# Graph network on one core: the logarithms of the edge counts are stored as they are computed, and the attention layers fetch them in pieces of 500 bytes

## The chip, the cores and the metric

The kernel runs on one core of one Trainium2 chip. The metric is the time of one execution in microseconds (us), as the device measures it. The unchanged kernel took 5342.97 us (median of 3 runs, 5340.74 to 5346.93).

## The reference

A graph of 3125 nodes with 256 features and 100,000 edges runs through two layers. Each layer has graph attention (four attentions in all), a linear attention, and a mixture of experts. What matters here is how every graph attention uses the edges:

```python
loop = jnp.arange(N)
src, dst = jnp.concatenate([src, loop]), jnp.concatenate([dst, loop])
e = leaky_relu(a_src[src] + a_dst[dst], 0.2)          # one number for each edge and head
ee = jnp.exp(e - segment_max(e, dst)[dst])
alpha = ee / (segment_sum(ee, dst)[dst] + 1e-16)
out = segment_sum(h[src] * alpha[:, :, None], dst)    # for each target node
```

An edge can occur several times, and each node has an edge to itself. The first attention has 4 heads of 64 features, the second and third 4 heads of 128, the fourth one head of 256.

## The kernel before

The kernel treats the graph as dense. It counts once how often each source node (3125) is tied to each target node (3125), and stores for each pair the negated logarithm of the count (a huge number where the count is 0) in the matrix `lowered` in device memory, `m.NL`, 3125 x 3125 float32, 39 MB. Node numbers are split as N = 3125, R = 125 rows to a tile, T = 25 tiles; W5 = 5.

*The counts stage* (`stage_counts`) goes through 25 tiles of 125 target nodes. For a tile it handles 25 windows of 5 target nodes. VectorE writes one-hot matrices (L303, four comparisons a tile), TensorE multiplies them (L317, L320) into PSUM banks, ScalarE takes the logarithm (L336) and a marker for zero (L337), and VectorE subtracts the two (L296) into `nl`, one of two buffers. There partition p stands for one of the window's five target nodes and one of 25 blocks of sources (p = 25 e + s), and along the row lie the 25 windows w with 125 sources b each. SyncE then stores `nl` with `tile_dma` (L65 for 112 partitions, L66 for the other 13) through the view `m.NLQ`. The view puts each run of 125 numbers (500 bytes) where a plain matrix has it: target node 5 (25 t + w) + e, sources 125 s + b. ScalarE may write into a buffer again when its store has landed (semaphore `nl_out`).

*The attention stages* (`stage_gat_attend`; in the trace g0a, g1a, g2a, g3a) go over the 25 tiles of target nodes, for two heads at a time (g3: one). So g0, g1 and g2 go through the tiles twice, g3 once: 50 + 50 + 50 + 25 = 175 fetches. A unit is one tile and one head. For a unit VectorE adds the scores (L932) into one of three buffers `x`, then adds the fetched rows `nl` and takes the minimum of each row in one instruction (L937, seen as CUSTOM_DVE_ANT_0), ScalarE takes exponentials (L991), TensorE transposes (L1102), ScalarE copies (L999), and TensorE gathers with the features (L1115). GpSimd finishes the rows; in g1 and g2 it stores them to `attended`.

`nl` has two buffers, for tiles of even and odd number. `counts` in the SyncE program of the stage fetches one tile: 125 rows of 12,500 bytes, one for each target node, on semaphore `nl_in`, which rises by 32 for the two transfers. SyncE issues the first two fetches at the start of the stage, and the fetch for tile t + 2 when both heads of tile t have been masked (semaphore `masked`). VectorE waits for `nl_in` ahead of L937 on the first head of a tile, after L932. SyncE does nothing else in these stages.

The order of work is written out by hand. The queues are in program order on each engine; all engines meet between stages.

Of the kernel before, what the change touches and what calls it, by code (L numbers as in the profile page):

```python
# [11 lines left out]
ds = bass.ds  # L12

N = 3125
R = 125
T = N // R
# [46 lines left out]
def tile_dma(eng, dst, src, sem):  # L63

    eng.dma_start(dst[0:CUT], src[0:CUT]).then_inc(sem, 16)  # L65
    eng.dma_start(dst[CUT:R], src[CUT:R]).then_inc(sem, 16)  # L66


def wait_apart(eng, tick, sem, value):

    eng.wait_ge(sem, value)
    eng.sem_inc(tick, 1)
# [20 lines left out]
W5 = 5  # L93
# [727 lines left out]
TURN = 6  # L821


def stage_gat_attend(nc, m, g, AL, HX, OUT, X=None, spare=None):
# [5 lines left out]
    H, F, HG = g.heads, g.feat, min(g.heads, 2)  # L830
# [3 lines left out]
    with Stage(nc, g.name + "a") as s:  # L834
        als, nl = s.sb("als", [R, H, N]), s.sb("nl", [R, 2, N])
# [10 lines left out]
        nl_in = [s.sem(f"nl_in{p}") for p in range(2)]  # L846
# [19 lines left out]
        def unit(q, i, k):  # L866
            return q * UT + i * BODY + k

        def tile_of(q, i, k):
            return q * T + i * TURN + k // HG  # L870

        def ahead(q, i, k, n):
            k += n
            if isinstance(i, int):
                at = i * BODY + k
                if at >= UT:
                    q, at = q + 1, at - UT
                i, k = at // BODY, at % BODY
                if i >= LOOPED:
                    i, k = LOOPED, at - LOOPED * BODY  # L880
            return q, i, k

        def exists(q, i, k, n):
            return not isinstance(i, int) or q * UT + i * BODY + k + n < PASSES * UT

        def before_all(q, i, k):
            return isinstance(i, int) and tile_of(q, i, k) < 0

        def ring(q, k):
            return (q * UT + k) % 3  # L890
# [7 lines left out]
        def units(eng, step, peeled=False):  # L898
            for q in range(PASSES):
                if q == 0 and peeled:  # L900
                    for k in range(BODY):
                        step(0, 0, k)
                with eng.Fori(1 if q == 0 and peeled else 0, LOOPED) as i:
                    for k in range(BODY):
                        step(q, i, k)
                for k in range(UT - LOOPED * BODY):
                    step(q, LOOPED, k)

        @block.sync
        def _(sp):  # L910
            def counts(gt, p):
                t = gt - gt // T * T if isinstance(gt, int) else gt
                tile_dma(sp, nl[:, p, :], m.NL[ds(t * R, R)], nl_in[p])
            counts(0, 0)
            counts(1, 1)
            for q in range(PASSES):
                with sp.Fori(0, T // 2 - 1) as i:
                    for p in range(2):
                        wait_apart(sp, s.tick, masked, (q * T + i * 2 + p + 1) * HG)
                        counts(i * 2 + p + 2, (q + p) % 2)  # L920
                for t in range(T - 3, T):
                    if q * T + t + 2 < PASSES * T and (t == T - 3 or q < PASSES - 1):
                        sp.wait_ge(masked, (q * T + t + 1) * HG)
                        counts(q * T + t + 2, (q + t) % 2)

        @block.vector
        def _(dve):
            def score(q, i, k):
                b, j, t = ring(q, k), k % HG, i * TURN + k // HG
                h = q * HG + j  # L930
                dve.wait_ge(turned, unit(q, i, k) * NG + NG)
                nc.vector.scalar_tensor_tensor(out=x[:, b, :], in0=als[:, h, :], scalar=cd[:, h:h + 1, ds(t, 1)].rearrange("p a b -> p (a b)"),  # L932
                                               in1=as2[:, j, :], op0=ALU.add, op1=ALU.min)
                nc.vector.drain()
                if j == 0:
                    wait_apart(dve, s.tick, nl_in[(q + k // HG) % 2], (i * TURN // 2 + (q * T + k // HG) // 2) * 32 + 32)
                nc.vector.tensor_tensor_reduce(out=x[:, b, :], in0=x[:, b, :], in1=nl[:, (q + k // HG) % 2, :], scale=1.0, scalar=3e38,  # L937
                                               op0=ALU.add, op1=ALU.min, accum_out=top[:, b:b + 1])
                nc.vector.drain().then_inc(masked, 1)  # L939

            def first(q, k):
                if q == 0:
                    dve.wait_ge(als_ready, (k + 1) * NG)
                    nc.vector.tensor_scalar(as2[:, k, :], als[:, k, :], 0.2, None, ALU.mult)
                    nc.vector.drain()
                else:
                    dve.wait_ge(scaled, (q - 1) * HG + k % HG + 1)
                score(q, 0, k)

            def invert(q, i, k):  # L950

                p = (q + k // HG) % 2
                dve.wait_ge(copied, (tile_of(q, i, k) + 1) * HG + 2)
                nc.vector.reciprocal(rec[:, p, :], raw[:, p, :, F]).then_inc(inverted, 1)

            dve.wait_ge(offset_ready, 1)
            for k in range(2):
                if k < HG:
                    first(0, k)
                else:  # L960
                    score(0, 0, k)
            dve.sem_inc(copied, 2)

            def step(q, i, k):
                if exists(q, i, k, 2):
                    nq, ni, nk = ahead(q, i, k, 2)
                    if nq > q and nk < HG:
                        first(nq, nk)
                    else:
                        score(nq, ni, nk)  # L970
                if (k - 2) % HG == HG - 1 and not before_all(q, i, k - 2):
                    invert(q, i, k - 2)
            units(dve, step, True)
            left = UT - LOOPED * BODY
            for k in range(left, left + 2):
                if (k - 2) % HG == HG - 1:
                    invert(PASSES - 1, LOOPED, k - 2)
# [1430 lines left out]
def build(nc, a, out):  # L2408
    m = Machine()
    m.src, m.dst = a["src"], a["dst"]  # L2410

    def dram(name, shape, dt=F32):
        return nc.dram_tensor(name, shape, dt).ap()
    m.QB = dram("edge_codes", [EDGES + CAP, 2])
    m.LO = dram("window_starts", [25, 25], I32)
    m.NL = dram("lowered", [N, N])
    m.NLQ = m.NL.rearrange("d s -> (d s)").rearrange("(t w p b) -> p t w b", t=T, w=T, p=R)
    m.XR, m.YR = dram("routed_rows", [SLOTS, D]), dram("expert_rows", [SLOTS, D])
    m.Y, m.XS = dram("attended", [N, 512]), dram("kept_rows", [R, T, D])
    with ExitStack() as ctx:  # L2420
# [150 lines left out]
```

## Time and profile before

| | before |
|---|---|
| median of 3 runs | 5342.97 us |
| lowest to highest | 5340.74 to 5346.93 us |
| profiled execution | 5338.39 us |
| its span | 5336.7 us |
| counts stage, first to last store issued | 174.6 to 446.7 us |
| g0 attention, first fetch to last mask | 926 to 1773 us |
| g1 and g2 | 2740 to 3572, 3729 to 4562 us |
| g3 | 4667 to 4992 us |
| busy in the span | TensorE 85%, VectorE 60%, ScalarE 53%, GpSimd 28% |

Times in rows of the profile are counted from the span's start. PE is TensorE's multiplications, PEld its loading of weights, DVE VectorE, ACT ScalarE, POOL GpSimd, SP SyncE; a q behind an engine's name means its sequencer, where transfers are issued. The DMA share is the mean busy share of the core's 16 DMA engines, and it can read slightly over 1. A row of windows gives the stretch, its length, the busy time of PE, PEld, DVE, ACT and POOL in this order with the number of instructions, TensorE's granted clock as a share of full speed, the DMA share and the GB/s moved. A row of the timeline gives start, duration, engine, line, operation, output and inputs, and in brackets the idle time before it and what ended it; of a tile's view, the shortest/median/longest duration in ns and the first and last start.

### The profile page before, as it was taken

What the parts mean: (1) busy time and instruction counts of PE and PEld (TensorE: products, weight loads), DVE (VectorE), ACT (ScalarE), POOL (GpSimd) and SP (SyncE); (2) the same over time, 40 slices, a digit from 0 to 9 for tenths busy, and PEclk for the clock granted to TensorE, in tenths of its full rate; (3) what the DMA queues carried; (4) which work ended last, traced back from release to release, by engine and by line L of the source; (5) the groups of instructions that cost most, each with busy time, mean ns of one, the idle gap of its engine ahead of it and who ended that gap; (6) DMA issues with size and microseconds to landing.
All of it is one profiled execution on the core that took longest, in us unless ns stands there. A gap on an engine that the chain in (4) does not pass through costs nothing. (4 is left out here: it accounts for less than half of the span.)

```text
span 5336.7 us, 91286 instructions
## 1 busy us (share of the span) xinstructions
PE 4535.1 (85%) x33942; PEld 4121.6 (77%) x33942; DVE 3198.2 (60%) x2773; ACT 2849.9 (53%) x3865; POOL 1473.4 (28%) x1158
## 2 busy tenths in 40 slices
PE   1554769999999629992979999997999999789989
PEld 1443447999999619991569999996999999778755
DVE  4896230788888521114458888862888888355333
ACT  0563322677777404431237787771777877344332
POOL 3001000122222040004016666660466666200000
PEclk9877769899999759996989999998999999899989
DMA  2583010333333045552024444422444344354100
GB/s 48 98 139 64 5 72 13 89 99 95 92 98 95 28 123 179 181 169 60 25 77 103 103 102 103 103 69 73 106 106 106 97 106 105 86 141 117 40 16 20
DMA packets 212208, 473.47 MB, mean 89 GB/s; under 512 B 117707, under 2 KB 160017, under 8 KB 188980
## 3 DMA queue, kind: packets, MB, share of 16 engines
q1 hardware_dynamic: 180420, 433.19, 31.6%
q0 software_dynamic: 22720, 27.06, 2.4%
q10 hardware_dynamic: 8736, 8.39, 0.5%
q8 instruction: 257, 4.21, 0.4%
q14 instruction: 75, 0.61, 0.0%
HBM read 388.23 MB, written 80.15 MB: 88 GB/s over the span
## 5 line engine op out<-in xcount | busy, mean ns | idle before, releaser
L1115 PE MATMUL g2a_pso<-HX,g2a_wt 125*125 125x129 f32 x5000 | 603.0, 274 | 6.1 <-ACT g2a_wt L999 3.3
L1115 PE MATMUL g1a_pso<-HX,g1a_wt 125*125 125x129 f32 x5000 | 602.8, 274 | 4.4 <-ACT g1a_wt L999 3.3
L1115 PE MATMUL g0a_pso<-HX,g0a_wt 125*125 125x65 f32 x5000 | 595.7, 274 | 5.8 <-ACT g0a_wt L999 3.3
L1115 PEld LDWEIGHTS g0a_pso<-HX,g0a_wt 125*125 125x125 f32 x5000 | 585.8, 193 | 6.3 <-ACT g0a_wt L999 3.5
L1115 PEld LDWEIGHTS g2a_pso<-HX,g2a_wt 125*125 125x125 f32 x5000 | 576.7, 189 | 6.5 <-ACT g2a_wt L999 3.5
L1115 PEld LDWEIGHTS g1a_pso<-HX,g1a_wt 125*125 125x125 f32 x5000 | 576.5, 189 | 4.9 <-ACT g1a_wt L999 3.5
L999 ACT ACTIVATE g0a_wt<-g0a_pst 125x1000 f32<-125x1000 f32 (+1 forms) x300 | 312.3, 1041 | 199.4 <-PE g0a_pst L1102 199.4
L932 DVE SCALAR_TENSOR_TENSOR g0a_x<-g0a_als,g0a_cd,HX 125x3125 f32<-125x3125 f32 x100 | 347.5, 3475 | 111.4 <-PE g0a_pst L1102 102.2
L932 DVE SCALAR_TENSOR_TENSOR g1a_x<-g1a_als,g1a_cd,g1a_as 125x3125 f32<-125x3125 f32 x100 | 358.5, 3585 | 81.1 <-PE g1a_pst L1102 70.9
L932 DVE SCALAR_TENSOR_TENSOR g2a_x<-g2a_als,g2a_cd,g2a_as 125x3125 f32<-125x3125 f32 x100 | 358.3, 3583 | 79.7 <-PE g2a_pst L1102 69.6
L999 ACT ACTIVATE g2a_wt<-g2a_pst 125x1000 f32<-125x1000 f32 (+1 forms) x300 | 312.4, 1041 | 169.2 <-PE g2a_pst L1102 169.2
L999 ACT ACTIVATE g1a_wt<-g1a_pst 125x1000 f32<-125x1000 f32 (+1 forms) x300 | 312.3, 1041 | 169.0 <-PE g1a_pst L1102 169.0
L937 DVE CUSTOM_DVE_ANT_0 g2a_x<-g2a_x,g2a_nl 125x3125 f32<-125x3125 f32 x100 | 344.5, 3445 | 20.7 <-issue 15.1
L937 DVE CUSTOM_DVE_ANT_0 g1a_x<-g1a_x,g1a_nl 125x3125 f32<-125x3125 f32 x100 | 344.7, 3447 | 19.6 <-issue 13.9
L937 DVE CUSTOM_DVE_ANT_0 g0a_x<-g0a_x,g0a_nl 125x3125 f32<-125x3125 f32 x100 | 341.6, 3416 | 19.6 <-issue 13.9
L1102 PE MATMUL g0a_pst<-C,g0a_x 125*125 125x125 f32 x2500 | 346.1, 284 | 3.6 <-ACT g0a_x L991 3.6
L991 ACT ACTIVATE g2a_x<-g2a_x,g2a_top 125x1000 f32<-125x1000 f32 (+1 forms) x300 | 346.6, 1156 | 2.9 <-DVEq L939 2.9
L991 ACT ACTIVATE g0a_x<-g0a_x,g0a_top 125x1000 f32<-125x1000 f32 (+1 forms) x300 | 346.7, 1156 | 2.4 <-DVEq L939 2.4
L991 ACT ACTIVATE g1a_x<-g1a_x,g1a_top 125x1000 f32<-125x1000 f32 (+1 forms) x300 | 346.5, 1156 | 1.5 <-DVEq L939 1.4
L1102 PE MATMUL g1a_pst<-C,g1a_x 125*125 125x125 f32 x2500 | 322.9, 273 | 3.6 <-ACT g1a_x L991 3.6
L1102 PE MATMUL g2a_pst<-C,g2a_x 125*125 125x125 f32 x2500 | 322.7, 273 | 2.2 <-ACT g2a_x L991 2.2
L1102 PEld LDWEIGHTS g0a_pst<-C,g0a_x 125*125 125x125 f32 x2500 | 305.6, 194 | 3.8 <-ACT g0a_x L991 3.8
(434 smaller groups left out, 8199.6 us busy)
## 6 DMA issues: line engine op xcount, KB each, us to landing
g0a_nl<-lowered SPq DMA_DIRECT2D x50, 1367.2 KB
g1a_nl<-lowered SPq DMA_DIRECT2D x50, 1367.2 KB
g2a_nl<-lowered SPq DMA_DIRECT2D x50, 1367.2 KB
moe_wa<-in_L_ffn_W SPq DMA_DIRECT2D x56, 1024.0 KB, 4.9
lowered<-counts_nl SPq DMA_DIRECT2D x25, 1367.2 KB
g3a_nl<-lowered SPq DMA_DIRECT2D x25, 1367.2 KB
g0a_nl<-lowered SPq DMA_DIRECT2D x50, 158.7 KB
g1a_nl<-lowered SPq DMA_DIRECT2D x50, 158.7 KB
```

The source lines that it names most:

```text
L932: nc.vector.scalar_tensor_tensor(out=x[:, b, :], in0=als[:, h, :], scalar=cd[:, h:h + 1, ds(t, 1)].rearrange("p a b -> p (a b)"), in1=as2[ ...
L937: nc.vector.tensor_tensor_reduce(out=x[:, b, :], in0=x[:, b, :], in1=nl[:, (q + k // HG) % 2, :], scale=1.0, scalar=3e38, op0=ALU.add, op1 ...
L991: nc.scalar.activation(x[:, b, c0:c1], x[:, b, c0:c1], ACT.Exp, bias=top[:, b:b + 1], scale=-1.0).then_inc(exped, 1)
L999: nc.scalar.activation(wt[:, side, 0:n * R].rearrange("p (b n) -> p b n", b=banks), pst[0:R, 3 * side:3 * side + banks, 0:per * R], ACT.Co ...
L1102: last = nc.tensor.transpose(pst[0:R, 3 * side + j // per, col:col + R], x[:, ring(q, k), (a0 + j) * R:(a0 + j + 1) * R], m.ident[0:R, 0:R])
L1115: last = nc.tensor.matmul(pso[0:R, unit(q, 0, k) % 2, 0:F + 1], wt[:, side, j * R:(j + 1) * R], HX[:, a, q * HG + k % HG, :], start=(a == ...
```

## The change

The stores and the fetches use another order of `lowered` in device memory. The counts stage now stores each partition's 25 runs one behind the other, 12,500 bytes for each of 125 partitions. The order within a tile is then e, s, w, b. For a tile the attention stages issue five transfers, one for each e. Each fills every fifth partition, 25 in all, from 25 x 25 runs of 125 numbers (500 bytes): partition 5 w + e gets source block s from the run s, w. The semaphore rises by 16 for each, 80 for a tile, and the waits follow. The number of bytes is the same, and so is what lands in `nl`.

```diff
         def _(sp):
             def counts(gt, p):
                 t = gt - gt // T * T if isinstance(gt, int) else gt
-                tile_dma(sp, nl[:, p, :], m.NL[ds(t * R, R)], nl_in[p])
+                for e in range(W5):
+                    sp.dma_start(nl[e:R:W5, p, :].rearrange("p (s b) -> p s b", s=T), m.NLD[ds(t, 1), e].rearrange("o w s b -> (o w) s b")).then_inc(nl_in[p], 16)
...
                 if j == 0:
-                    wait_apart(dve, s.tick, nl_in[(q + k // HG) % 2], (i * TURN // 2 + (q * T + k // HG) // 2) * 32 + 32)
+                    wait_apart(dve, s.tick, nl_in[(q + k // HG) % 2], (i * TURN // 2 + (q * T + k // HG) // 2) * (16 * W5) + 16 * W5)
...
     m.NL = dram("lowered", [N, N])
-    m.NLQ = m.NL.rearrange("d s -> (d s)").rearrange("(t w p b) -> p t w b", t=T, w=T, p=R)
+    m.NLQ = m.NL.rearrange("d s -> (d s)").rearrange("(t p w b) -> p t w b", t=T, w=T, p=R)
+    m.NLD = m.NL.rearrange("d s -> (d s)").rearrange("(t e s w b) -> t e w s b", t=T, e=W5, s=T, w=T)
```

## Rows read from the trace of the kernel before

**Rows 1.** Windows: stretch, us, busy by engine (instructions), granted clock, DMA share, GB/s.

```profile
926.00:1773.00 847.00, 836.15 (x7411) 834.21 (x7412) 701.10 (x349) 645.91 (x701) 190.71 (x142) 0.97 0.36 93
2740.00:3572.00 832.00, 822.50 (x7414) 820.73 (x7415) 715.37 (x349) 662.10 (x748) 503.14 (x328) 0.99 0.41 102
4667.00:4992.00 325.00, 309.88 (x1686) 275.18 (x1687) 177.69 (x98) 154.75 (x161) 12.87 (x22) 0.96 0.47 121
```

**Rows 2.** Waits in 2740:3572: who for whom, total us, times, longest.

```profile
DVE g1a_x L932 <- PE g1a_pst L1102: 70.9, 89, 1.2
DVE g1a_x L937 <- issue: 13.9, 50, 0.4
```

**Rows 3.** One fetch of g1 in the timeline, and a window on it.

```profile
2990.77 0.32 SPq L65 DMA_DIRECT2D g1a_nl<-lowered  x1
3007.23 0.32 SPq L65 DMA_DIRECT2D g1a_nl<-lowered  x1
...
2987.07 3.42 DVE L937 CUSTOM_DVE_ANT_0 g1a_x<-g1a_x,g1a_nl 125x3125 f32<-125x3125 f32 x1
3012.22 3.43 DVE L937 CUSTOM_DVE_ANT_0 g1a_x<-g1a_x,g1a_nl 125x3125 f32<-125x3125 f32 x1 [0.32 <-issue]
...
2991.00:2998.00 7.00, 7.00 (x67) 7.00 (x66) 6.07 (x2) 5.45 (x7) 4.02 (x5) 1.00 0.91 229
```

**Rows 4.** Counts stage: waits in 200:420, all stores, instructions near 300.

```profile
ACT counts_ln L336 <- DMA lowered<-counts_nl: 71.4, 18, 5.4
DVE counts_nl L296 <- ACTq L338: 17.7, 14, 2.2
...
L65 SPq DMA_DIRECT2D lowered<-counts_nl x25: 322/322/328, 174.6 to 446.7; - x25
...
299.96 4.66 SPq L66 DMA_DIRECT2D lowered<-counts_nl  x1
...
311.25 0.68 ACT L336 ACTIVATE counts_ln<-counts_ps,counts_neg 125x500 f32<-125x500 f32 x1 [4.81 <-DMA lowered<-counts_nl]
```

**Rows 5.** Timeline and windows: loads of 125 rows as issued and running.

```profile
4.78 0.34 SPq L123 DMA_DIRECT2D codes_srci<-in_src  x1
5.17 0.30 SPq L124 DMA_DIRECT2D codes_dsti<-in_dst  x1
...
8.00:10.00 2.00, 0.00 (x0) 0.00 (x0) 0.00 (x0) 0.00 (x0) 0.00 (x0) 1.00 0.32 131
10.00:12.00 2.00, 0.00 (x0) 0.00 (x0) 0.00 (x0) 0.00 (x0) 0.00 (x0) 1.00 0.32 130
...
73.51 1.05 SPq L65 DMA_DIRECT2D X<-in_x  x1
...
74.00:75.00 1.00, 0.00 (x0) 0.00 (x0) 0.00 (x0) 0.47 (x1) 0.00 (x0) 1.00 0.32 2
```

**Rows 6.** Windows: 500-byte stores, the counts stage, 512-byte loads.

```profile
311.00:312.00 1.00, 1.00 (x16) 0.93 (x15) 1.00 (x2) 0.75 (x2) 0.00 (x0) 1.00 1.02 274
312.00:313.00 1.00, 0.89 (x13) 0.68 (x10) 1.00 (x1) 1.00 (x3) 0.00 (x0) 1.00 1.02 235
200.00:400.00 200.00, 113.15 (x985) 95.91 (x986) 183.81 (x89) 130.76 (x247) 0.00 (x0) 0.74 0.86 138
5128.00:5129.00 1.00, 0.00 (x0) 0.00 (x0) 0.59 (x3) 0.00 (x0) 0.00 (x0) 0.50 1.01 296
```

**Rows 7.** Tile views: first and last start of fetches and score instructions.

```profile
L65 SPq DMA_DIRECT2D g0a_nl<-lowered x50: 313/317/343, 926.2 to 1740.2; - x50
...
L932 DVE SCALAR_TENSOR_TENSOR g0a_x<-g0a_als,g0a_cd,HX x100: 3472/3474/3491, 933.3 to 1765.9; 125x3125 f32<-125x3125 f32 x100
L937 DVE CUSTOM_DVE_ANT_0 g0a_x<-g0a_x,g0a_nl x100: 3412/3416/3419, 937.0 to 1769.5; 125x3125 f32<-125x3125 f32 x100
...
L65 SPq DMA_DIRECT2D g3a_nl<-lowered x25: 313/317/333, 4667.9 to 4964.1; - x25
L937 DVE CUSTOM_DVE_ANT_0 g3a_x<-g3a_x,g3a_nl x25: 3414/3415/3418, 4679.8 to 4987.8; 125x3125 f32<-125x3125 f32 x25
```

## The prediction, on record before the changed kernel was run

> **What bounds the kernel now.** I read the page's first two parts, then the busy time by stage, then the waits of a stage, then single instructions. The span is 5336.7 us inside a profiled execution of 5338.4 us, 0.09% under the median of the runs, 5342.97 us; my sum is made on 5338.4. Over half of it is the four attention stages, 847 us for g0, 832 for g1, as much for g2, which repeats g1's row, and 325 for g3; in each of them TensorE is busy 95% to 99% of the time [rows 1]. They fetch 50, 50, 50 and 25 tiles of `lowered`. Nobody waits for these fetches: in the list of waits of the g1 stage the DMA `g1a_nl` doesn't appear, VectorE waits for TensorE, and the masking instruction of L937 has 0.3 us of "issue" ahead of it [rows 2].
>
> How much cover has a fetch? One is issued at 2990.77, when the second head of its buffer's old tile is masked. Its own tile is masked first at 3012.22, so it has 21.3 us to land, and a tile takes 3007.23 - 2990.77 = 16.46 us [rows 3]. Today the sixteen DMA engines move it in about 7 us (share 0.91 over 2991 to 2998) [rows 3], and nothing shows. The chain of waits reaches back only over the last stage, so it is of no use here.
>
> In the counts stage ScalarE waits for the stores of `lowered`: 71.4 us in 18 waits between 200 and 420 us, while VectorE waits only 17.7 us [rows 4]. The rhythm is (446.7 - 174.6)/24 = 11.34 us a tile [rows 4].
>
> **Part 1, the stores.** 3125 pieces of 500 bytes a tile become 125 of 12,500 bytes. The new store is shaped like today's fetch: about 7 us [rows 3] against the 11 to 12 us from a store's issue to ScalarE's restart (299.6 to 311.25; L65 is issued 0.36 us ahead of the L66 row) [rows 4]. What is late next is VectorE: busy 183.81 of 200 us, its four comparisons and one subtraction come to 0.919 x 11.34 = 10.4 us a tile; ScalarE's work is 130.76/200 x 11.34 = 7.4 us [rows 6], which leaves TensorE 3 us to fill the first bank. So 24 x (11.34 - 10.4) = 23 us, and some 3 us at the end of the stage, where the next one waits for the last store. It can't be more, since VectorE has no idle time left, and it is 0 if the long writes should be as slow as the short ones. I take -25 us.
>
> **Part 2, the fetches: which engines.** A tile is now five transfers of 25 partitions x 25 runs of 500 bytes. The page lists no 25-row load big enough to see; nearest are loads of 125 rows. The two index loads of 390.6 KB, issued together at 4.78 and 5.17 us, hold the DMA share at 0.32 for four microseconds: 5 of 16 engines, at 131/5 = 26 GB/s each [rows 5]. Two transfers in flight had the same five engines, otherwise the share would be 0.63. The fetch of 125 x 5 single words shows 0.32 again, so it is no matter of size [rows 5]. 112 rows use all sixteen (share about 1 at 2991 to 2998). The bounds for 25 rows are therefore: all sixteen engines, or five and the same five for all five transfers. I take five, as 25 like 125 splits evenly into five, not into sixteen.
>
> The Trainium skill, "DMA: Bandwidth & Descriptors", in "Why a DMA increments its semaphore by 16 and not by 1", says that a transfer gets the largest number up to 16 that divides the slowest dimension of both sides, and on this path always the lowest-numbered engines. The index loads agree (125 gives 5, share 0.32); for 25 it gives 5 as well, and no run here shows that yet. By it the sum is the forecast; with sixteen engines it would be the first rival.
>
> **Part 2, the fetches: what a piece costs.** 3125 pieces on five engines are 625 on each. Per piece and engine, from share x 16 x bytes / GB/s: loads of 512-byte runs take 1.01 x 16 x 512/296 = 28.0 ns; the 500-byte stores take 1.02 x 16 x 500/274 = 29.8 ns in their first microsecond, 34.7 ns in the next, and over the stage 0.86 x 16 x 500/138 = 50 ns, when sixteen engines crowd the memory [rows 6]. Five engines at 500 bytes in 29 ns move 86 GB/s, less than the 131 GB/s that the same five moved [rows 5], so I take the uncrowded 29 ns. 28 and 50 ns are the ends.
>
> 625 x 29 ns = 18.1 us a tile: it no longer fits into the 16.46 us that a tile takes, and the engines, not the cover, set the rhythm. Latency doesn't add: in this state a tile's two maskings end 10.7 us after it lands (3.42 for L937, 3.47 for the next score's L932, 3.42 again and 0.4 between them [rows 7]), so the next fetch is queued before the five engines are done with the one between. In g1 and g2 GpSimd's stores of `attended` load the same engines: (0.41 x 832 - 0.36 x 847)/50 = 0.7 us a tile more than in g0 [rows 1], so 18.8 us.
>
> From a stage's first fetch to the end of its last mask, new: 2 us of latency + tiles x rhythm + 10.7 us (3.4 with one head), against old [rows 7]:
> - g0: 12.7 + 50 x 18.1 = 918, old 1772.9 - 926.2 = 847: +71
> - g1: 12.7 + 50 x 18.8 = 953, old 832 [rows 1]: +121
> - g2 the same: +121
> - g3: 5.4 + 25 x 18.1 = 458, old 4991.2 - 4667.9 = 323: +135
>
> Together +448; g3 is hit hardest per tile, since its tile has one head and takes only 12.8 us. The wait that appears is VectorE's, ahead of L937 on the first head of a tile. Behind it on VectorE stand the reciprocal of the tile before and all later scores; TensorE and ScalarE run dry behind it. Each nanosecond of piece cost is 0.625 x 175 = 109 us.
>
> **Costs put at nothing.** SyncE issues five transfers instead of two. An issue takes 0.32 us, but one behind a transfer of many pieces waits until those are generated: 4.66 us behind 2800 pieces [rows 4], thus some 5.5 us a tile. SyncE has nothing else to do in these stages, and 5.5 is under 18. If generating were bound to the number of engines, the word fetch bounds it: 625 words held back the next issue by about 1 us [rows 5]. The bigger wait value costs nothing.
>
> Sum: 5338.4 - 25 + 448 = 5761, so about 5760 us.
>
> The skill's same page, "Specifications", wants at least 512 bytes for full rate and has a read-modify-write below. Here 500 bytes in 29.8 ns against 512 in 28.0 show little of it; the forecast would stay.
>
> **Rivals.**
> - *All sixteen engines share a fetch* (the other side: faster). 195 pieces an engine at 29 to 50 ns are 6 to 10 us, inside 21.3 us of cover, and all that is left is the faster counts stage: 5338 - 25 = 5313 us. It decides as soon as a fetch takes below 16.4 us of engine time, that is from six or more engines. For it: 112 rows do use sixteen. Against: both five-engine rows [rows 5].
> - *The crowded rate*, 50 ns: 31.3 us a tile, 21 ns x 109 = 2300 us more: about 8050 us. For it: the only 500-byte pieces in the trace average that. Against: they were writes to memory by sixteen engines at once, and began at 29.8. A middling 34.7 ns gives 6390 us.
> - *The cheapest piece*, 27 ns: 16.9 us a tile nearly fits g0 (+10), adds 60 in g1 and in g2, and 104 in g3: 5547 us. A little cheaper still and only g3 is late, +100 us at most.
> - *TensorE's clock falls in its new idle time*: in the counts stage, with TensorE busy 57%, the granted clock is 0.74 [rows 6]; g3 would have it busy some 70%, so 12.8/0.74 = 17.3 us a tile, still inside 18.1. It adds nothing unless the clock goes lower.
>
> **How the numbers follow.** Five engines at 27 to 31 ns a piece: 0.63, and 5760 us is its middle. Five engines at 31 to 35 ns: 0.17. Dearer: 0.10. Five engines and below 27 ns: 0.03. Sixteen engines: 0.06, faster; no difference (within 0.2%, which is about what a measurement of this kernel can tell): 0.01. So slower 0.93. The range goes from 5530 to 6400 us and leaves out the crowded rate and the sixteen engines, 0.16 to 0.2 together.
>
> **What would show it.** In the new trace: the DMA share in the attention stages near 0.31, nearly without gaps, at some 85 GB/s; SyncE issuing every 18 to 19 us in all four stages, g3 too; VectorE waiting for the DMA `nl` at L937 on every second score (every one in g3), TensorE's busy share below 95%; in the counts stage no wait of ScalarE for `lowered` and 10.4 us a tile. I am wrong if the share is near 1 in short bursts (sixteen engines), or if a piece takes another time than 28 to 30 ns: then the rhythm says which.

## The result and the profile after

The changed kernel takes 5417.98 us (median of 4 runs, 5416.93 to 5422.84) against 5341.85 us of the kernel before in the same comparison: ratio 1.0148, 95% interval 1.0129 to 1.0166. That is 76 us slower, where about 420 were forecast; 5418 lies under the range, which began at 5530. The profiled execution has a span of 5415.3 us, 78.6 us longer than before.

From the page of the changed kernel: the DMA share in 40 slices and the packets.

```profile
DMA  2341011333332245530133333322333333433200
...
DMA packets 661510, 473.47 MB, mean 87 GB/s; under 512 B 585757, under 2 KB 628068, under 8 KB 657031
```

The bytes are those of before, the packets three times as many. The DMA row stands at an even 3 where the attention stages are.

The same kernel by windows (the counts stage, then g0, g1 and g3 from first fetch to last mask), with the columns of [rows 1]:

```profile
200.00:400.00 200.00, 120.97 (x1090) 102.80 (x1091) 200.00 (x98) 144.21 (x266) 0.00 (x0) 0.79 0.46 150
897.00:1739.00 842.00, 823.67 (x7428) 821.73 (x7429) 704.30 (x349) 646.40 (x702) 194.87 (x142) 0.98 0.36 94
2705.00:3559.00 854.00, 831.05 (x7464) 827.78 (x7465) 709.60 (x350) 665.38 (x752) 594.62 (x328) 0.99 0.37 100
4666.00:5088.00 422.00, 348.15 (x1779) 303.30 (x1780) 177.60 (x98) 158.47 (x168) 69.74 (x22) 0.91 0.36 93
```

Against [rows 1]: g0 842 us (847 before), g1 854 (832), g2 855 (833), g3 422 (325). In the counts stage VectorE is now busy all the time, against 183.81 of 200 us in [rows 6]. The waits name the cause:

```profile
DVE g3a_x L938 <- DMA g3a_nl<-lowered: 233.2, 25, 10.5
DVE g2a_x L938 <- DMA g2a_nl<-lowered: 95.0, 47, 7.9
```

In g3 every tile waits, in g2 47 of 50, in g1 43 and in g0 32. The timeline of g3 shows one tile of VectorE and, in one merged row, SyncE held for 13 transfers without a break:

```profile
4799.36 3.42 DVE L938 CUSTOM_DVE_ANT_0 g3a_x<-g3a_x,g3a_nl 125x3125 f32<-125x3125 f32 x1 [10.48 <-DMA g3a_nl<-lowered]
...
4799.16 43.28 SPq L914 DMA_DIRECT2D g3a_nl<-lowered  x13
```

43.28/13 = 3.33 us a transfer, 16.6 us a tile, where a tile of g3 took 12.8 us [rows 7]. First and last starts, as in [rows 4] and [rows 7]:

```profile
L65 SPq DMA_DIRECT2D lowered<-counts_nl x25: 321/322/337, 174.1 to 422.2; - x25
...
L914 SPq DMA_DIRECT2D g3a_nl<-lowered x125: 796/3112/4092, 4666.1 to 5074.0; - x125
L938 DVE CUSTOM_DVE_ANT_0 g3a_x<-g3a_x,g3a_nl x25: 3412/3415/3417, 4684.8 to 5083.8; 125x3125 f32<-125x3125 f32 x25
```

The stores go at (422.2 - 174.1)/24 = 10.34 us a tile, and g3's maskings are (5083.8 - 4684.8)/24 = 16.63 us apart.

Where the 78.6 us are, from first fetch to first fetch in the two traces:

| stretch | before | after | difference |
|---|---|---|---|
| start to g0's first fetch | 926.2 | 897.1 | -29.1 |
| g0 to g1 | 1813.9 | 1807.9 | -6.0 |
| g1 to g2 | 989.7 | 1005.3 | +15.6 |
| g2 to g3 | 938.1 | 955.8 | +17.7 |
| g3 to the end of the span | 668.8 | 749.2 | +80.4 |

### The profile page after: what moved, and what is told of

Its sections match the earlier page's. It is cut to its first block and busy times, and to the rows that moved or that the text cites. A ratio compares the mean times of both kernels' runs of the same rounds, so it can differ in the third digit from the quotient of the medians.

```text
span 5415.3 us, 92735 instructions
## 1 busy us (share of the span) xinstructions
PE 4545.3 (84%) x33942; PEld 4120.4 (76%) x33942; DVE 3191.0 (59%) x2773; ACT 2848.9 (53%) x3865; POOL 1668.8 (31%) x1158
## 5 line engine op out<-in xcount | busy, mean ns | idle before, releaser
L1116 PEld LDWEIGHTS g2a_pso<-HX,g2a_wt 125*125 125x125 f32 x5000 | 576.0, 189 | 15.6 <-ACT g2a_wt L1000 10.9
L1116 PE MATMUL g3a_pso<-HX,g3a_wt 125*125 125x257 f32 x1250 | 305.3, 400 | 54.7 <-ACT g3a_wt L1000 43.3
```

The lines of the kernel that those rows point to most:

```text
L1116: last = nc.tensor.matmul(pso[0:R, unit(q, 0, k) % 2, 0:F + 1], wt[:, side, j * R:(j + 1) * R], HX[:, a, q * HG + k % HG, :], start=(a == ...
```

## The experiments

The ratios are to the kernel before in the same comparison (median 5328.97 us in the first four, 5329.47 us in the others); the difference of two medians can say 0.1% more or less than the ratio. Where the number of transfers changes, the waits follow it; those lines of the edits aren't shown.

**1. The fetch cut into 16 and 9 partitions.** The part with 16 follows the table of rules in "DMA: Bandwidth & Descriptors" of the Trainium skill ("Rules for kernel authors"), which asks for a multiple of 16 in the outermost dimension to use all engines.

```diff
                 for e in range(W5):
-                    sp.dma_start(nl[e:R:W5, p, :].rearrange("p (s b) -> p s b", s=T), m.NLD[ds(t, 1), e].rearrange("o w s b -> (o w) s b")).then_inc(nl_in[p], 16)
+                    src = m.NLD[ds(t, 1), e].rearrange("o w s b -> (o w) s b")
+                    for w0, w1 in ((0, 16), (16, T)):
+                        sp.dma_start(nl[e + w0 * W5:e + (w1 - 1) * W5 + 1:W5, p, :].rearrange("p (s b) -> p s b", s=T), src[w0:w1]).then_inc(nl_in[p], 16)
```

> The change with each of a tile's five transfers cut in two, 16 and 9 partitions, same bytes, same 3125 pieces of 500 bytes, 10 transfers. Theory (pieces on the busiest engine set the rhythm, 26.6 ns each): 16 rows use 16 engines and 9 rows use 9, so the busiest has 5 x (25 + 25) = 250 pieces, 6.6 us a tile, hidden behind 16.4 us; what is left is the faster counts stage, 24.5 + 4.6 us: about 5313 us against 5342 of the kernel before, and VectorE never waits for nl. Rival (SyncE is held 3.33 us for each transfer because making 625 descriptors takes that long, whatever the engines): 3125 pieces still take 16.6 us a tile, g3 stays at 16.6 us, total about 5417 us.

Measured: 5310.15 us, ratio 0.9968 (0.9956 to 0.9980): 19 us faster than the kernel before, and 1.8% faster than the change (0.9968/1.0148). Its g3, first as maskings, then the only wait for `nl` among its longest 200, then as a window:

```profile
L940 DVE CUSTOM_DVE_ANT_0 g3a_x<-g3a_x,g3a_nl x25: 3412/3415/3418, 4648.4 to 4956.7; 125x3125 f32<-125x3125 f32 x25
...
DVE g3a_x L940 <- DMA g3a_nl<-lowered: 3.9, 3, 2.1
...
4636.00:4961.00 325.00, 309.88 (x1687) 275.63 (x1688) 177.65 (x97) 154.79 (x162) 12.94 (x22) 0.96 0.51 121
```

12.85 us a tile as before, and 121 GB/s as in [rows 1]. The same 3125 pieces are hidden once they lie on more engines. The limit isn't the number of pieces that SyncE has to make. That more than nine engines work at once is an estimate from one microsecond of this g3, 4736 to 4737: it moves 246 GB/s, where five engines of the change move at most 105 in a microsecond of theirs (4813 to 4814), 21 each.

**2. Whole rows on five engines.** The order in memory and the stores of the kernel before; five transfers of 25 rows of 12,500 bytes.

```diff
-                tile_dma(sp, nl[:, p, :], m.NL[ds(t * R, R)], nl_in[p])
+                rows = m.NL[ds(t * R, R)].rearrange("(w e) s -> w e s", e=W5)
+                for e in range(W5):
+                    sp.dma_start(nl[e:R:W5, p, :], rows[:, e]).then_inc(nl_in[p], 16)
```

> The kernel before's order in memory and its stores, but the fetch as five transfers of 25 whole rows of 12,500 bytes (rows 5w + e). Theory: five engines, 25 rows each, at 26 GB/s an engine 0.48 us a row, so 12.0 us a tile: under 12.8 us of g3 and 16.4 us of the others, so the same as before, 5342 us within 0.2%, VectorE waiting little or not at all for nl. Rival (that a fetch uses only five engines, or is five transfers, costs by itself): g1, g2 and g3 slower as in the change, up to 5445 us (5417 plus the 29 us that the stores gave).

Measured: 5334.51 us, ratio 1.0018 (1.0006 to 1.0030). Nearly no loss. In its trace two places show a fetch of 12 to 13 us that isn't covered: g3 waits 35.0 us in 10 waits, and the first mask of each stage comes 15 us after its first fetch instead of 11 or 12. From g3's first fetch to the end of the span are 676.6 us against 668.8. (The profiled execution took 5358 us, 24 more than the median, and 14 of them lie between g0's first fetch and g1's; the last section comes back to that.)

```profile
DVE g3a_x L939 <- DMA g3a_nl<-lowered: 35.0, 10, 4.8
```

So five engines alone do not make the change's loss, nor five transfers: it takes the short pieces as well.

**3. The store alone.** The new view `m.NLQ` with the fetch of the kernel before.

```diff
-    m.NLQ = m.NL.rearrange("d s -> (d s)").rearrange("(t w p b) -> p t w b", t=T, w=T, p=R)
+    m.NLQ = m.NL.rearrange("d s -> (d s)").rearrange("(t p w b) -> p t w b", t=T, w=T, p=R)
```

> The change's store and the kernel before's fetch; what lands in nl is in another order, so the part left out is putting the pieces in place. Theory: the counts stage at 10.3 us a tile as in the change (first to last store 248 us against 272), attention as before: 5342 - 29 = 5313 us. Rival (the counts stage gains nothing by itself, the 29 us are an effect of the fetches or of the start of g0): 5342 us.

Measured: 5307.64 us, ratio 0.9956 (0.9942 to 0.9970), 21 us in the medians; its profiled span is 28.7 us shorter. Stores from 174.0 to 422.1 us. The first part of the prediction holds by itself. Run 1 reaches the same time within a few us, so its fetch costs next to nothing.

**4. The cut at 21 and 4.** As run 1 with `((0, 21), (21, T))`.

> As the run with 16 and 9, but 21 and 4 partitions. Theory: 21 rows use 7 engines (75 pieces each) and 4 rows use 4 (25 each), so the busiest engines have 5 x 100 = 500 pieces: 500 x 26.6 ns = 13.3 us a tile. That is hidden in g0, g1 and g2 and just over the 12.8 us of g3: g3's maskings 13.3 us apart, total 5313 + 0 to 15, about 5320 us. Rival (descriptor making): 16.6 us, 5417 us.

Measured: 5335.30 us, ratio 1.0011 (1.0000 to 1.0023), where the expected 5320 of 5342 us would be 0.996. The rhythm of g3 came nearly as expected, the time didn't.

```profile
L940 DVE CUSTOM_DVE_ANT_0 g3a_x<-g3a_x,g3a_nl x25: 3412/3416/3418, 4670.2 to 4998.0; 125x3125 f32<-125x3125 f32 x25
```

g3 goes at 13.66 us a tile: 27.3 ns for each of 500 pieces on the busiest engines, against 26.6 ns for each of 625 in the change. What the expectation left out is the start of each stage, where a fetch has no cover: the first mask comes 17 to 18 us after the first fetch, where run 1 has 12. In the traces this run is 26 us longer than run 1, 17 us of them between the first fetches of g0 and g3 and 10 from there on. The rhythm follows the pieces on the busiest engine, and the rival that making them sets it (16.6 us whatever the split) falls. Both splits agree with the rule of the Trainium skill that the prediction named ("DMA: Bandwidth & Descriptors", "Why a DMA increments its semaphore by 16 and not by 1"): 25 rows use 5 engines, 21 use 7, 16 use 16.

**5. Pieces of 100 bytes on the same five engines.**

```diff
+                    src = m.NLH[ds(t, 1), e].rearrange("o w x y b -> (o w) x y b")
+                    sp.dma_start(nl[e:R:W5, p, :].rearrange("p (x y b) -> p x y b", x=R // W5, y=W5), src).then_inc(nl_in[p], 16)
...
+    m.NLH = m.NL.rearrange("d s -> (d s)").rearrange("(t e y w x b) -> t e w x y b", t=T, e=W5, y=W5, w=T, x=T)
```

> The change with pieces of 100 bytes instead of 500: the same five transfers of 25 partitions, the same bytes, 15,625 pieces a tile; the pieces land in another order, so putting them in place is left out. Theory (an engine's time for a piece is a fixed part and a part by bytes; 100-byte stores took 11 to 13 ns each in the kernel before's records): 3125 pieces on each of five engines at 12 ns are 37.5 us a tile in every attention stage, about 2513 + 175 x 37.5 = 9075 us. Rival (each piece costs the same 26.6 ns or is limited where it is made): 83 us a tile, about 17,000 us. Rival (bytes alone count): 16.6 us a tile, 5417 us.

Measured: 7738.67 us, ratio 1.4528 (1.4499 to 1.4558). All three figures missed; the first came nearest.

```profile
L939 DVE CUSTOM_DVE_ANT_0 g3a_x<-g3a_x,g3a_nl x25: 3414/3415/3416, 6688.8 to 7403.1; 125x3125 f32<-125x3125 f32 x25
...
6800.00:7100.00 300.00, 161.33 (x750) 137.63 (x750) 70.92 (x40) 65.34 (x70) 31.55 (x10) 0.76 0.43 53
```

29.76 us a tile for 3125 pieces on an engine: 9.5 ns each. With 26.6 ns for 500 bytes, the straight line through the two is 5.2 ns and 0.043 ns a byte. A piece costs neither the same whatever its size nor by its bytes alone. If making the pieces had set the change's 16.6 us a tile, that is 5.3 ns for each of 3125, making 15,625 would have taken 83 us. The expected 12 ns had come from how long records of 100 bytes last. The window's share says the same here, 0.43 x 16 x 100/53 = 13.0 ns, and the rhythm says 9.5: five engines are 0.31 of sixteen, so the records of one engine overlap, and share overstates the price of a piece.

**6 and 7. The cut in g3 alone, and in all but g3.**

```diff
+    CUTS = ((0, 16), (16, T)) if HG == 1 else ((0, T),)      # run 7: if HG == 2
...
+                    for w0, w1 in CUTS:
```

> The change with the cut into 16 and 9 partitions in g3 alone. Theory: of the change's 78.6 us over the kernel before, 80 belong to g3 (from its first fetch to the end of the span 749.2 us against 668.8), so 5417 - 80 = 5337 us on the scale of the kernel before's 5342, which is about no difference to it; g1 and g2 stay at 16.8 us a tile. Rival (the loss is in g0 to g2, the 97 us by which g3's maskings end later being slack): 5400 us or more.

> The mirror of the last: cut in g0, g1 and g2, whole in g3. Theory: g1 and g2 give back 15.6 + 17.7 us and their cover, g0 nothing, so 5417 - 27 to -33, about 5387 us, 1.0085 of the kernel before; g3's maskings stay 16.6 us apart. Rival: 5340 us.

Measured: 5337.63 us, ratio 1.0023 (1.0012 to 1.0035), and 5385.90 us, ratio 1.0110 (1.0093 to 1.0127), a little over the expected 1.0085. Cutting g3 takes 1.0148 to 1.0023, cutting the others takes it to 1.0110. Run 1 stands at 0.9968, so g3 alone costs 1.42% (76 us) and g0 to g2 together 0.55% (29 us). Added to 0.9968 that makes 1.0165, at the upper end of the interval of the change's 1.0148. Counted down from the change instead, g3 is worth 1.25% (67 us) and the others 0.38% (20 us). In run 6 g1 and g2 stay at 16.8 us a tile and wait as in the change (g1 89.5 us in 48 waits):

```profile
DVE g2a_x L941 <- DMA g2a_nl<-lowered: 96.0, 47, 7.7
```

**8. The kernel before with its short stores on five engines.**

```diff
-                tile_dma(sp, m.NLQ[:, t], nl[:, t % 2], nl_out[t % 2])
+                for e in range(W5):
+                    sp.dma_start(m.NLQ[e * T:(e + 1) * T, t], nl[e * T:(e + 1) * T, t % 2]).then_inc(nl_out[t % 2], 16)
```

> The kernel before with each tile's store of 500-byte pieces issued as five transfers of 25 partitions instead of 112 and 13; fetches as before. It measures the disputed price on its own, for writes: 625 pieces on each of five engines. If a piece costs what it costs the change's fetches (26.6 ns), the counts stage goes at 16.6 us a tile, 24 x (16.6 - 11.3) = +127 us, 1.024 of the kernel before. At the 29 ns of my prediction: 18.1 us a tile, +163 us, 1.031. At the crowded 50 ns: 31 us, +480 us, 1.09.

Measured: 5537.36 us, ratio 1.0397 (1.0377 to 1.0416), above all but the crowded figure. The counts stage by windows, and SyncE held for 12 transfers:

```profile
200.00:600.00 400.00, 138.09 (x1174) 115.86 (x1175) 219.66 (x105) 153.74 (x291) 0.00 (x0) 0.66 0.36 82
...
247.34 45.84 SPq L345 DMA_DIRECT2D lowered<-counts_nl  x12
```

45.84/12/125 = 30.6 ns a piece, and by bytes x engines/rate 500 x 5/82 = 30.5 ns. On five engines, at 82 GB/s in all, a 500-byte write costs 30.5 ns where the change's reads, 500 x 5/93, cost 26.9 ns. Two things differ besides the direction: these transfers take 25 neighbouring partitions, the change's every fifth, and they run in another stage. Run 2 fetches into every fifth partition too and lands its whole rows in time, so the spacing isn't known to cost or save anything.

## Why the prediction was wrong

The mechanism was right at each main step. The term that failed is the price of a piece, 29 ns where 26.6 were measured; two smaller terms and the end of the sum missed as well.

- *Stores, -25 us*: right. 10.34 us a tile and 29.1 us less up to g0's first fetch; run 3 by itself 21 us in the medians.
- *Five engines, the same for all five transfers*: right. 93 GB/s at a share of 0.36 in g3, and runs 1 and 4 move the rhythm as the division of the rows says. The rival of sixteen engines falls.
- *The engines set the rhythm and VectorE waits ahead of the masking*: right, SyncE without a pause, 25 waits in g3. That g3 is hit hardest was right too (run 6). TensorE's share fell below 95% in g3 alone.
- *29 ns a piece*: this is the step that failed. It came to 26.6 ns (16.63 us a tile over 625 pieces on each engine). I had taken it from the 500-byte stores in their uncrowded microsecond (29.8 ns), with the 512-byte loads (28.0 ns) as the lower end, and called the difference from 50 ns crowding. Run 8 points at what I missed, the direction: 500-byte writes cost 30.5 ns on five engines alone, near my 29.8, and the change's reads are cheaper. The 512-byte loads were the nearer row. That it is the direction alone wasn't tried apart from the partitions. I had also multiplied by the share, which reads too high: the change's five engines show 0.36 to 0.37, where 5/16 is 0.31, so records of one engine overlap. Without that factor the loads give 16 x 512/296 = 27.7 ns, and that microsecond may not have been full.
- *The multiplier*. I had written that each nanosecond is worth 109 us. 2.4 ns are then 263 us, three quarters of the miss. The rhythm of 16.6 us fell almost upon TensorE's own 16.46 us, where g0 to g2 pay the small difference of two large numbers. "Below 27 ns" had a chance of 0.03, though the nearer row reads 27.7 to 28.0.
- *0.7 us a tile for the stores of `attended`* in g1 and g2: it was 16.8 - 16.6, near 0.2 us. The same difference of shares in the change's rows, (0.37 x 854 - 0.36 x 842)/50, gives 0.26; that before it had counted the stores' waiting among sixteen crowded engines is my reading and wasn't tried. That is 2 x 50 x 0.5 = 50 us of the miss.
- *The end of the last mask as the end of a stage*: this left out the drain. With the measured rhythms my own formula gives -29 - 4 + 21 + 21 + 98 = +107 us, and +78.6 was measured. The traces show why. Before, VectorE ran ahead of TensorE by the three buffers `x`; starved, TensorE follows close behind. In g3 the last masking's row accumulation starts at 4991.12 us before and TensorE ends at 5031.78, 40.7 us later; in the change it is 5087.16 and 5110.96, 23.8 us. So 17 us of the delay come back in g3, and 5 to 6 in each of g1 and g2 by the table above. These are VectorE's last row accumulation and TensorE's last line in g3, before and then after:

```profile
4991.12 0.08 DVE L937 DVE_READ_ACCUMULATOR2_ANT g3a_top<- 125x1 f32 x1
...
5024.66 7.12 PE L1115 MATMUL g3a_pso<-HX,g3a_wt 125*125 125x257 f32 x32
```

```profile
5087.16 0.08 DVE L938 DVE_READ_ACCUMULATOR2_ANT g3a_top<- 125x1 f32 x1
...
5103.84 7.12 PE L1116 MATMUL g3a_pso<-HX,g3a_wt 125*125 125x257 f32 x32
```

- *SyncE's issuing, put at nothing*: it cost nothing, but I had read the 4.66 us behind 2800 pieces [rows 4] as the time of making them, 5.5 us a tile. In the change SyncE is held 3.33 us for a transfer of 625 pieces, in run 1 0.78 us (median in g0) for one of 400 or 225. The hold goes with the pieces on one engine, 125 and 25, and not with the number made.

The forecast's 448 us of loss in attention become 448 - 263 - 50 - 28 = 107; less the 29 us of the counts stage that is 78 us.

The rival of the crowded rate is out: 3125 pieces on five engines reach 94 GB/s at 26.6 ns a piece, not 50. The rival of the falling clock added nothing to g3's rhythm, since VectorE waited for every fetch: g3 had a granted clock of 0.91 with TensorE busy 82% of the time.

## What to carry to other kernels

Where a change puts a resource close to the rhythm of the bound, the error of one unit price decides the whole result; price the piece from a row with the same direction and size, take bytes x engines/rate over a full window, and let the range reach across the point where the resource stops to bind. Count the first fetch of each stage, which nothing covers (run 4). Count a transfer's rows: 25 or 125 rows run on five engines, and cutting 25 into 16 and 9 turned the same layout from 1.5% slower into 0.3% faster (run 1, the fastest here that leaves nothing out). Time a stage to the end of its slowest engine, not of the engine that waits, since a starved pipeline drains faster.

## What the runs showed of the hardware

- A piece costs an engine about 5.2 ns and 0.043 ns a byte when read in pieces of 100 and 500 bytes; writes of 500 bytes cost 4 ns more (run 8). The line goes through these two sizes only: 0.043 ns a byte would hold an engine under 24 GB/s, and the index loads reach 131/5 = 26 [rows 5]. The Trainium skill, "DMA: Bandwidth & Descriptors", "Specifications", wants 512 bytes for full rate; here reads of 500 bytes reach 93/5 = 18.6 GB/s an engine, and loads of 512 bytes, on sixteen engines at once, 296/16 = 18.5 [rows 6]. The index loads with their 26 GB/s have rows of 3200 bytes (390.6 KB in 125 rows), so 512 bytes don't reach the full rate here, and no step shows just below them.
- g0 came out 6 us shorter in spite of the slower fetch. Its TensorE starts idling earlier in the stage, goes to half clock earlier and comes back earlier. In windows of 10 us the granted clock is 0.50 from 946 to 986 before, where TensorE is busy 7.5 to 10 us of each; in the change it is 0.50 only from 917 to 937, where TensorE is busy 3.9 and 7.9 us of 10. Two more windows of 10 us, 50 us after g0's first fetch, before and then after:

```profile
976.00:986.00 10.00, 10.00 (x50) 10.00 (x49) 2.38 (x2) 4.48 (x5) 0.00 (x0) 0.50 0.00 1
```

```profile
947.00:957.00 10.00, 10.00 (x94) 10.00 (x94) 8.71 (x4) 7.49 (x9) 0.00 (x0) 1.00 0.37 100
```

Both are busy throughout, one at 1.2 and one at 2.4 GHz. Run 6 repeats the 6 us (1807.7 us from g0's first fetch to g1's), and run 1, without starvation, has 1813.3. That the clock is the cause was read from the traces and not tried by itself, and run 4, which starts its stage starved too, has 1820.2.
- Executions with the same fetches differ in this stretch by more than 6 us. Run 7's g0 is that of run 1 and takes 1823.8 us. Where the stage goes over to its second pair of heads TensorE stands about 3 us in both; then run 1 goes on at full clock (94 multiplications in 1345 to 1355, granted clock 1.00) and run 7 at half:

```profile
1346.00:1356.00 10.00, 10.00 (x49) 10.00 (x49) 5.13 (x4) 4.47 (x5) 1.15 (x3) 0.50 0.23 56
```

Run 2 does the same in 1367 to 1377 (x49, 0.50), with 1827.8 us for the stretch. Why the clock falls there in one execution and not in another stays open. A single profile of this kernel doesn't settle a difference of some 10 us.
